# x load behind the zero fills, four first scatters on one table, one key wait per chunk, and a new penalty and reload order in the first attention

## The chip, the cores and the metric

The kernel runs on one core of a Trainium2 chip. The metric is device microseconds (us) of one execution, lower is better; three runs give a median, and one further execution was profiled. The engines are named as in the profile: PE (matmul), PEld (its weight load), DVE, ACT, POOL, and SP, which only issues transfers; SPq and ACTq are the queues that these two issue on.

## What is computed

Node features `x` (1024 x 512) pass four residual blocks: a graph attention, a mixture of 8 experts, a graph convolution, and a transformer layer with experts of its own. The graph has 17408 edges (`src`, `dst`, self loops included). The change is in the first block and in the making of its adjacency matrix:

```
x = x + L0_gnn(layernorm(x))
q, k, v = xn @ Wq + bq, xn @ Wk + bk, xn @ Wv + bv
adj  = zeros(1024, 1024).at[src, dst].set(1.0)
a    = q @ k.T / sqrt(512)
a    = a * adj + (1 - adj) * (-1e6)
out  = softmax(a) @ v
```

The third block needs the number of times that each edge occurs (`segment_sum` over repeated edges), so the kernel makes counts once and keeps them in DRAM.

## The kernel before

**Edges.** Edge e lies at partition p, column c (136 columns, in 34 "quads" of 4). A key `src * 1024 + dst` is compared with those of the same column on PE and DVE (`quad`), which turns an edge that occurs twice in a column into one leader with a count; `leaders` writes `index` and `count` for 2 quads at a time (the first 10 quads) or 3 quads at a time (the other 24) and raises `edges_ready` by that number. Each column is then one indirect transfer of 128 values that POOL issues (L447) and that adds `count` into a table of 1024 x 1024 floats in DRAM. There are two tables, so that a transfer need only wait for the one before the last: column c goes to table c % 2 and waits until column c - 2 has landed (`scattered[r]`). A table is cleared by a 4 MB transfer of zeros (L265) and a 512-byte one for a spare row (L267), both on SP's queue; `tables_clear[r]` counts them. SP's queue holds, in order: src, dst, the zeros of table 0, its spare row, the zeros of table 1, its spare row, two biases, four weight blocks. ACT issues the load of x as its first instruction.

**Projections.** DVE first does 10 quads, then waits for x, takes the layernorm (L795 to L820), and the halves of the first weights (WL). PE transposes the normalised x (L1213), then does the projections, with 3 quads ahead of each of 8 column blocks, and the scores q k^T, which ACT writes to `SR` (L573). Sums are made of three products of split operands (L237).

**First attention.** After the last scatter SP loads rows of both tables, 128 rows of the matrix (a tile t) at a time, into `CT[:, par, 0]` and `CT[:, par, 1]`, par = t % 2 (L321, `count_in`). POOL adds them (L474, `summed`), then makes the penalty 1e6 * min(count, 1) in `CT[:, par, 1]` (L476, `penalty`). DVE: m1 = min(count, 1) * SR (L908), m2 = (penalty - 1e6) + m1 (L913), the row maximum (L916). ACT: exp (L619). PE transposes the result (L1281), ACT copies that (`p_hi`, PTH), DVE takes the rest (`p_lo`, PTL, L787), PE multiplies with v (`values`), DVE adds to x (`residual`, L931) and takes statistics. The order on DVE is mask(t+2), p_lo(t+1), residual(t); on ACT softmax(t+2), p_hi(t+1). SP stores the summed counts (L325, `count_out`, `stored`) and loads tile t + 2 into the buffers of tile t once exp(t) and the store of t are done:

```
                wait(A["summed"], 2 * i + par + 1)
                count_out(2 * i + par, par)
                wait(A["exp"], 2 * i + par + 1)
                wait(A["stored"], 32 * i + 16 * par + 16)
                count_in(2 * i + par + 2, par)
```

Of the kernel before, what the change touches and what calls it, by code (L numbers as in the profile page):

```python
# [21 lines left out]
ALU = mybir.AluOpType  # L22
ACT = mybir.ActivationFunctionType
# [3 lines left out]
P = 128  # L27
# [6 lines left out]
def build(nc, a, out, ctx):  # L34
# [5 lines left out]
    EC = NE // P  # L40
# [3 lines left out]
    NH, DH = 8, D // 8  # L44
    NEG = 1000000.0
    TABLES = 2
    QUADS = EC // 4
    assert EC % 4 == 0 and HB == 2 and GB == 8 and NT == 8 and KT == 4

# [197 lines left out]
    def _(sp):  # L247
        def wait(s, value):

            sp.wait_ge(s, value)  # L250
            if not isinstance(value, int):
                sp.nop(nofuse=True)
# [11 lines left out]
        for r in range(TABLES):  # L264
            sp.dma_start(tables[r][0:N * N, :].rearrange("(p c f) o -> p c (f o)", p=P, c=4),  # L265
                         zeros[:, :].unsqueeze(1).to_broadcast([P, 4, 2048])).then_inc(tables_clear[r], 16)
            sp.dma_start(tables[r][N * N:N * N + P, :], zeros[:, 0:1]).then_inc(tables_clear[r], 16)  # L267
        with nc.allow_non_contiguous_dma(reason="biases, one feature per partition"):
            sp.dma_start(bq0[:, :], a["L0_gnn_bq"].rearrange("(k p) -> p k", p=P)).then_inc(cols0_in, 16)
            sp.dma_start(bk0[:, :], a["L0_gnn_bk"].rearrange("(k p) -> p k", p=P)).then_inc(cols0_in, 16)  # L270
# [43 lines left out]


        for r in range(TABLES):
            wait(scattered[r], 32 * QUADS)

        def count_in(t, par):
            for r in range(TABLES):  # L320
# [9 lines left out]
        with sp.Fori(0, NT // 2 - 1) as i:  # L330
            for par in range(2):
                wait(A["summed"], 2 * i + par + 1)
                count_out(2 * i + par, par)
                wait(A["exp"], 2 * i + par + 1)
                wait(A["stored"], 32 * i + 16 * par + 16)
                count_in(2 * i + par + 2, par)
        for t in (NT - 2, NT - 1):
# [74 lines left out]
    def _(gp):  # L412
# [23 lines left out]
                allow_small_or_imprecise_dtypes=True).then_inc(setup, 1)  # L436


        for r in range(TABLES):
            wait(tables_clear[r], 32)  # L440
        for q in range(QUADS):
            wait(edges_ready, q + 1)
            for c in range(4 * q, 4 * q + 4):
                r = c % TABLES
                if c >= TABLES:
                    wait(scattered[r], 16 * (c // TABLES))
                gp.indirect_dma_start(  # L447
                    out=tables[r], out_offset=bass.IndirectOffsetOnAxis(ap=index[:, c:c + 1], axis=0),
                    in_=count[:, c:c + 1], in_offset=None, compute_op=ALU.add).then_inc(scattered[r], 16)
# [20 lines left out]
        with gp.Fori(0, NT // 2) as i:  # L470
            for par in range(2):
                t = 2 * i + par
                wait(A["c_in"][par], 32 * i + 32)
                gp.tensor_tensor(CT[:, par, 0, :], CT[:, par, 0, :], CT[:, par, 1, :], ALU.add).then_inc(A["summed"], 1)  # L474
                wait(A["summed"], t + 1)
                gp.tensor_scalar(CT[:, par, 1, :], CT[:, par, 0, :], 1.0, NEG, ALU.min, ALU.mult).then_inc(A["penalty"], 1)  # L476

        def moe_split(which, u0, skip_first):
            if not skip_first:
# [85 lines left out]
    def _(act):  # L565
# [22 lines left out]
            copy(WH[:, slot, :], RAW[:, raw, :], w_hi)  # L588


        act.dma_start(X[:, :, :], a["x"].rearrange("(t p) d -> p t d", p=P)).then_inc(x_in, 16)
        root(0)
        for u in range(4):
            w_hi_of(u, 0, u, u)
# [17 lines left out]
            copy(SR[:, t, :], banks(4 + 2 * (t % 2)), Q0["s_done"], scale=D ** -0.5)  # L612


        def softmax(half, par):
            t = 2 * half + par
            act.wait_ge(A["mx"], t + 1)
            act.wait_ge(A["t_ps"][par], half)
            act.activation(PR[:, par, :], CT[:, par, 3, :], ACT.Exp, bias=neg_max[:, par:par + 1],  # L619
                           accum_out=denom[:, par:par + 1]).then_inc(A["exp"], 1)  # L620

        def p_hi(half, par):
            act.wait_ge(A["t_ps"][par], half + 1)
            act.wait_ge(A["av_ps"][par], half)
            copy(PTH[:, par, :], banks(4 + 2 * par), A["t_hi"][par])

        softmax(0, 0)
        softmax(0, 1)
        p_hi(0, 0)
        with act.Fori(0, NT // 2 - 1) as i:  # L630
            softmax(i + 1, 0)
            p_hi(i, 1)
            softmax(i + 1, 1)
            p_hi(i + 1, 0)
        p_hi(NT // 2 - 1, 1)
# [148 lines left out]
    def _(v):  # L784
# [118 lines left out]
        def mask(half, par):  # L903

            t = 2 * half + par
            v.wait_ge(A["summed"], t + 1)
            v.wait_ge(Q0["s_done"], NT)
            v.scalar_tensor_tensor(out=CT[:, par, 2, :], in0=CT[:, par, 0, :], scalar=1.0,  # L908
                                   in1=SR[:, ds(t), :].rearrange("p a n -> p (a n)"),
                                   op0=ALU.min, op1=ALU.mult).then_inc(A["m1"], 1)  # L910
            v.wait_ge(A["m1"], t + 1)
            v.wait_ge(A["penalty"], t + 1)
            v.scalar_tensor_tensor(out=CT[:, par, 3, :], in0=CT[:, par, 1, :], scalar=NEG, in1=CT[:, par, 2, :],  # L913
                                   op0=ALU.subtract, op1=ALU.add).then_inc(A["m2"], 1)
            v.wait_ge(A["m2"], t + 1)
            v.tensor_reduce(out=neg_max[:, par:par + 1], in_=CT[:, par, 3, :], axis=X_AXIS, op=ALU.max,  # L916
                            negate=True).then_inc(A["mx"], 1)
# [670 lines left out]
```

## Time and profile before

| | |
|---|---|
| three runs | 1388.9, 1382.31, 1389.77 us, median 1388.9 |
| profiled execution | 1383.41 us, span of its records 1381.6 us |
| busy share of the span | PE 77%, PEld 61%, DVE 49%, ACT 27%, POOL 49% |
| granted clock of PE, mean | 0.882 of full speed |

The busy shares are means over stages with different limits. No engine is busy all the time, so what a change in a stage is worth is read in that stage, from what each engine waits for there.

### The profile page before, as it was taken

To read this page: it belongs to the slowest core of one execution; us is meant where nothing else is said; L and a number is where in the kernel's file an instruction comes from. 1 tells how busy PE (TensorE), PEld (TensorE's weight loads), DVE (VectorE), ACT (ScalarE), POOL (GpSimd) and SP (SyncE) were. 2 spreads that over 40 slices of the span, in tenths; PEclk is the share of its full clock that TensorE was granted. 3 is DMA by queue.
4 is the path that set the end of the run, shared out by engine and by line. 5 is a ranking of instruction groups with operands and counts; after the bars stand their busy time and mean duration, and the time that the engine had idled before them with its cause. 6 is when DMAs were issued, how large, how long until landed. Compare 5 with 4: busy or idle time off the path is not lost.

```text
span 1381.6 us, 14502 instructions
## 1 busy us (share of the span) xinstructions
PE 1067.3 (77%) x4784; PEld 837.3 (61%) x4784; DVE 682.7 (49%) x1231; ACT 369.8 (27%) x536; POOL 670.7 (49%) x429
## 2 busy tenths in 40 slices
PE   3576797003878999995889878999998754999994
PEld 2455685002654788884678656777776633588883
DVE  6544320004763333455512466777877777243448
ACT  0201111001223121212221036656665522212120
POOL 1687888887632243210532036776856633233430
PEclk9977799555887899997999979999999995899997
DMA  9534222224521011002321031010000031111101
GB/s 307 63 24 26 8 1 1 0 12 156 182 77 30 16 53 53 23 0 87 99 58 39 15 100 30 16 46 17 23 16 16 0 122 46 31 46 46 46 0 61
DMA packets 79841, 68.86 MB, mean 50 GB/s; under 512 B 32288, under 2 KB 63264, under 8 KB 78512
## 3 DMA queue, kind: packets, MB, share of 16 engines
q1 hardware_dynamic: 59168, 66.06, 16.5%
q0 software_dynamic: 19584, 0.08, 4.2%
q10 hardware_dynamic: 1040, 2.10, 0.5%
q8 instruction: 28, 0.46, 0.1%
q14 instruction: 21, 0.17, 0.0%
HBM read 47.17 MB, written 16.85 MB: 46 GB/s over the span
## 4 chain that ended last, share of the span: by engine, by line
PE 52%; DVE 18%; POOL 14%; issue 7%; DMA 6%; ACT 3%; SPq 0%; DVEq 0%; ACTq 0%; POOLq 0%
PE PS L237 40%; POOL edge_table L447 13%; DMA edge_table<-zeros 3%; DMA edge_table<-count,index 3%; DVE neg_max L1119 2%; PE PS L1452 2%; PE PS L1467 2%; PE PS L1441 2%; DVE APL L787 2%; PE PS L1466 2%; PE PS L1357 2%; DVE stats L795 1%; DVE XN L820 1%; DVE XN L1187 1%; PE PS L1213 1%
## 5 line engine op out<-in xcount | busy, mean ns | idle before, releaser
L459 POOL CAST WH<-RAW 128x512 fp32r<-128x512 f32 x94 | 65.5, 696 | 466.8 <-PE PS L237 370.1
L447 POOL DMA_INDIRECT edge_table<-count,index x136 | 214.9, 1580 | 87.0 <-issue 42.0
L537 POOL TENSOR_SCALAR AP__133<-AP__133,rden 128x1024 f32<-128x1024 f32 x64 | 181.9, 2847 | 84.9 <-DVE rden L1124 84.2
L237 PE MATMUL PS<-XTH,WH 128*128 128x512 f32 x480 | 169.8, 421 | 8.9 <-DVE XTL L787 6.7
L237 PE MATMUL PS<-XTL,WH 128*128 128x512 f32 x480 | 164.4, 409 | 0.0
L237 PE MATMUL PS<-XTH,WL 128*128 128x512 f32 x480 | 162.2, 404 | 0.0
L461 POOL TENSOR_TENSOR WL<-RAW,WH 128x512 fp32r<-128x512 f32 x94 | 138.2, 1470 | 12.1 <-POOL WH L459 0.8
L787 DVE TENSOR_TENSOR HL<-HF,HH 128x1024 fp32r<-128x1024 f32 x32 | 46.9, 1468 | 174.4 <-ACT HH L573 174.4
L237 PEld LDWEIGHTS PS<-XTH,WH 128*128 128x128 f32 x480 | 95.2, 201 | 32.8 <-issue 12.4
L237 PEld LDWEIGHTS PS<-XTL,WH 128*128 128x128 f32 x480 | 96.6, 201 | 20.8
L655 ACT ACTIVATE HF<-PS,b 128x1024 f32<-128x1024 f32 x32 | 35.7, 1117 | 272.0 <-PE PS L237 272.0
L237 PEld LDWEIGHTS PS<-XTH,WL 128*128 128x128 f32 x480 | 95.2, 198 | 21.4
L237 PE MATMUL PS<-WH,HH 128*128 128x512 f32 x256 | 99.6, 389 | 0.0
L237 PE MATMUL PS<-WL,HH 128*128 128x512 f32 x256 | 99.6, 389 | 0.0
L237 PE MATMUL PS<-WH,HL 128*128 128x512 f32 x256 | 99.6, 389 | 0.0
L1119 DVE TENSOR_REDUCE neg_max<-PS 128x1 f32<-128x1024 f32 x64 | 78.2, 1222 | 36.2 <-PE PS L1441 35.3
L787 DVE TENSOR_TENSOR APL<-PS,APH 128x512 fp32r<-128x512 f32 x128 | 82.9, 678 | 23.3 <-ACT APH L573 23.2
L1281 PE MATMUL PS<-ident,PR 128*128 128x128 f32 x64 | 11.2, 333 | 104.5 <-ACT PR L619 104.5
L573 ACT ACTIVATE APH<-PS 128x512 fp32r<-128x512 f32 x128 | 71.7, 597 | 67.4 <-PE PS L1452 43.0
L1213 PE MATMUL PS<-ident,XN 128*128 128x128 f32 x128 | 30.8, 417 | 67.1 <-DVE XTL L787 33.3
L1452 PE MATMUL PS<-ident,AP__133 128*128 128x128 f32 x512 | 70.8, 280 | 11.3 <-DVE APL L787 10.8
L1452 PEld LDWEIGHTS PS<-ident,AP__133 128*128 128x128 f32 x512 | 59.6, 143 | 26.9 <-issue 17.0
(189 smaller groups left out, 2013.1 us busy)
## 6 DMA issues: line engine op xcount, KB each, us to landing
edge_table<-zeros SPq DMA_DIRECT2D x2, 4096.0 KB, 28.0
RAW<-in_L_ffn_w SPq DMA_DIRECT2D x32, 256.0 KB, 2.7
CT<-edge_table SPq DMA_DIRECT2D x16, 512.0 KB, 5.0
RAW<-in_L_ffn_W SPq DMA_DIRECT2D x32, 256.0 KB, 2.8
counts<-CT SPq DMA_DIRECT2D x8, 512.0 KB, 6.0
CG<-counts SPq DMA_DIRECT2D x8, 512.0 KB, 3.3
RAW<-in_L_gnn_W SPq DMA_DIRECT2D x16, 256.0 KB, 2.7
edge_table<-count,index POOLq DMA_INDIRECT x136, 3.0
```

Source lines behind the costliest of these rows:

```text
L237: got = pe.matmul(o, lhs, r, start=first and j == 0, stop=last and j == 2)
L447: gp.indirect_dma_start(out=tables[r], out_offset=bass.IndirectOffsetOnAxis(ap=index[:, c:c + 1], axis=0), in_=count[:, c:c + 1], in_offse ...
L459: gp.tensor_copy(wh, RAW[:, raw, :]).then_inc(w_hi, 1)
L461: gp.tensor_tensor(wl, RAW[:, raw, :], f(wh), ALU.subtract).then_inc(w_ready, 1)
L537: gp.tensor_scalar(AP_[:, i % 4, :], AP_[:, i % 4, :], rden[:, i % 4:i % 4 + 1], None, ALU.mult).then_inc(B["norm"], 1)
L573: act.activation(dst, src, Copy, **kw).then_inc(s, 1)
L655: act.activation(HF[:, b, :], banks(2 * b), ACT.Gelu, bias=b1[:, ds(2 * e + b)]).then_inc(M["gelu"][b], 1)
L787: v.tensor_tensor(dst, src, f(hi), ALU.subtract).then_inc(s, 1)
L1119: v.tensor_reduce(out=neg_max[:, i % 4:i % 4 + 1], in_=banks(2 * (i % 2)), axis=X_AXIS, op=ALU.max, negate=True).then_inc(B["mx"], 1)
L1213: got = pe.transpose(PS[:, t % 2, k * P:(k + 1) * P], src[:, t, k * P:(k + 1) * P], ident[:, :])
L1357: pe.matmul(PS[:, 4 + t % 4, :], gatesT[0:NEXP, t * P:(t + 1) * P], b2[:, which, :], start=True, stop=True).then_inc(M["g_ps"], 1)
L1452: got = pe.transpose(PS[:, 4 + half, k * P:(k + 1) * P], AP_[:, i % 4, c * P:(c + 1) * P], ident[:, :])
```

## The change

1. The load of x is taken from ACT's queue and put on SP's, behind the zeros of both tables.
2. Columns 0 to 3 are all added into table 0; from column 4 on the tables alternate as before. The first transfer waits for table 0 alone, and column 5, the first of table 1, waits for that table. SP's two final counts follow (70 transfers on table 0, 66 on table 1).
3. POOL waits for `edges_ready` once for each group of 2 or 3 quads (13 waits), not at each of 34 quads.
4. The penalty is made by ACT as relu(1 - count), ahead of each exp, and DVE's m2 is now (relu * -1e6) + m1. DVE's m2(t) also waits for exp(t-2), which reads the buffer that it writes.
5. SP loads tile t + 2 after m2(t) in place of exp(t). The store of t is still waited for.

```diff
--- before.py
+++ after.py
@@ -44,6 +44,7 @@
     NH, DH = 8, D // 8
     NEG = 1000000.0
     TABLES = 2
+    FIRST = 4
     QUADS = EC // 4
     assert EC % 4 == 0 and HB == 2 and GB == 8 and NT == 8 and KT == 4
 
@@ -265,6 +266,7 @@
             sp.dma_start(tables[r][0:N * N, :].rearrange("(p c f) o -> p c (f o)", p=P, c=4),
                          zeros[:, :].unsqueeze(1).to_broadcast([P, 4, 2048])).then_inc(tables_clear[r], 16)
             sp.dma_start(tables[r][N * N:N * N + P, :], zeros[:, 0:1]).then_inc(tables_clear[r], 16)
+        sp.dma_start(X[:, :, :], a["x"].rearrange("(t p) d -> p t d", p=P)).then_inc(x_in, 16)
         with nc.allow_non_contiguous_dma(reason="biases, one feature per partition"):
             sp.dma_start(bq0[:, :], a["L0_gnn_bq"].rearrange("(k p) -> p k", p=P)).then_inc(cols0_in, 16)
             sp.dma_start(bk0[:, :], a["L0_gnn_bk"].rearrange("(k p) -> p k", p=P)).then_inc(cols0_in, 16)
@@ -314,7 +316,7 @@
 
 
         for r in range(TABLES):
-            wait(scattered[r], 32 * QUADS)
+            wait(scattered[r], 8 * (EC - FIRST) + 16 * FIRST * (1 - r))
 
         def count_in(t, par):
             for r in range(TABLES):
@@ -331,7 +333,7 @@
             for par in range(2):
                 wait(A["summed"], 2 * i + par + 1)
                 count_out(2 * i + par, par)
-                wait(A["exp"], 2 * i + par + 1)
+                wait(A["m2"], 2 * i + par + 1)
                 wait(A["stored"], 32 * i + 16 * par + 16)
                 count_in(2 * i + par + 2, par)
         for t in (NT - 2, NT - 1):
@@ -436,14 +438,17 @@
                 allow_small_or_imprecise_dtypes=True).then_inc(setup, 1)
 
 
-        for r in range(TABLES):
-            wait(tables_clear[r], 32)
+        into = [0] * FIRST + [c % TABLES for c in range(FIRST, EC)]
+        chunk_starts = set(range(0, 10, 2)) | set(range(10, QUADS, 3))
         for q in range(QUADS):
-            wait(edges_ready, q + 1)
+            if q in chunk_starts:
+                wait(edges_ready, q + 1)
             for c in range(4 * q, 4 * q + 4):
-                r = c % TABLES
-                if c >= TABLES:
-                    wait(scattered[r], 16 * (c // TABLES))
+                r, turn = into[c], into[:c].count(into[c])
+                if turn:
+                    wait(scattered[r], 16 * turn)
+                else:
+                    wait(tables_clear[r], 32)
                 gp.indirect_dma_start(
                     out=tables[r], out_offset=bass.IndirectOffsetOnAxis(ap=index[:, c:c + 1], axis=0),
                     in_=count[:, c:c + 1], in_offset=None, compute_op=ALU.add).then_inc(scattered[r], 16)
@@ -472,8 +477,6 @@
                 t = 2 * i + par
                 wait(A["c_in"][par], 32 * i + 32)
                 gp.tensor_tensor(CT[:, par, 0, :], CT[:, par, 0, :], CT[:, par, 1, :], ALU.add).then_inc(A["summed"], 1)
-                wait(A["summed"], t + 1)
-                gp.tensor_scalar(CT[:, par, 1, :], CT[:, par, 0, :], 1.0, NEG, ALU.min, ALU.mult).then_inc(A["penalty"], 1)
 
         def moe_split(which, u0, skip_first):
             if not skip_first:
@@ -588,7 +591,6 @@
             copy(WH[:, slot, :], RAW[:, raw, :], w_hi)
 
 
-        act.dma_start(X[:, :, :], a["x"].rearrange("(t p) d -> p t d", p=P)).then_inc(x_in, 16)
         root(0)
         for u in range(4):
             w_hi_of(u, 0, u, u)
@@ -612,6 +614,11 @@
             copy(SR[:, t, :], banks(4 + 2 * (t % 2)), Q0["s_done"], scale=D ** -0.5)
 
 
+        def no_edge(half, par):
+            t = 2 * half + par
+            act.wait_ge(A["summed"], t + 1)
+            act.activation(CT[:, par, 1, :], CT[:, par, 0, :], ACT.Relu, bias=1.0, scale=-1.0).then_inc(A["penalty"], 1)
+
         def softmax(half, par):
             t = 2 * half + par
             act.wait_ge(A["mx"], t + 1)
@@ -624,12 +631,16 @@
             act.wait_ge(A["av_ps"][par], half)
             copy(PTH[:, par, :], banks(4 + 2 * par), A["t_hi"][par])
 
+        no_edge(0, 0)
+        no_edge(0, 1)
         softmax(0, 0)
         softmax(0, 1)
         p_hi(0, 0)
         with act.Fori(0, NT // 2 - 1) as i:
+            no_edge(i + 1, 0)
             softmax(i + 1, 0)
             p_hi(i, 1)
+            no_edge(i + 1, 1)
             softmax(i + 1, 1)
             p_hi(i + 1, 0)
         p_hi(NT // 2 - 1, 1)
@@ -910,8 +921,9 @@
                                    op0=ALU.min, op1=ALU.mult).then_inc(A["m1"], 1)
             v.wait_ge(A["m1"], t + 1)
             v.wait_ge(A["penalty"], t + 1)
-            v.scalar_tensor_tensor(out=CT[:, par, 3, :], in0=CT[:, par, 1, :], scalar=NEG, in1=CT[:, par, 2, :],
-                                   op0=ALU.subtract, op1=ALU.add).then_inc(A["m2"], 1)
+            v.wait_ge(A["exp"], t - 1) if t >= 2 else None
+            v.scalar_tensor_tensor(out=CT[:, par, 3, :], in0=CT[:, par, 1, :], scalar=-NEG, in1=CT[:, par, 2, :],
+                                   op0=ALU.mult, op1=ALU.add).then_inc(A["m2"], 1)
             v.wait_ge(A["m2"], t + 1)
             v.tensor_reduce(out=neg_max[:, par:par + 1], in_=CT[:, par, 3, :], axis=X_AXIS, op=ALU.max,
                             negate=True).then_inc(A["mx"], 1)
```

How the change moves instructions is shown at three places. First SP's queue at the start of the program (the names are tiles and inputs; `zeros` is the source of the fills). Before:

```order
L265 DMA edge_table0<-zeros_98 512x1x2048 [waits zeros_set]
L267 DMA edge_table0<-zeros_98 128x1
L265 DMA edge_table1<-zeros_98 512x1x2048
L267 DMA edge_table1<-zeros_98 128x1
L269 DMA bq0_60<-in_L0_gnn_bq 128x4x1
L270 DMA bk0_61<-in_L0_gnn_bk 128x4x1
L258 DMA RAW_84<-in_L0_gnn_Wq 128x4x128
```

And in the changed kernel:

```order
L266 DMA edge_table0<-zeros_98 512x1x2048 [waits zeros_set]
L268 DMA edge_table0<-zeros_98 128x1
L266 DMA edge_table1<-zeros_98 512x1x2048
L268 DMA edge_table1<-zeros_98 128x1
L269 DMA X_87<-in_x 128x8x512
L271 DMA bq0_60<-in_L0_gnn_bq 128x4x1
L272 DMA bk0_61<-in_L0_gnn_bk 128x4x1
L259 DMA RAW_84<-in_L0_gnn_Wq 128x4x128
```

x is now the fifth transfer of that stretch, ahead of the biases and of every weight. Second, POOL at its first scatters. Before:

```order
L447 DMA edge_table0<-count_112,index_111 1048704x1 [waits edges_ready,table1_clear,table0_clear]
L447 DMA edge_table1<-count_112,index_111 1048704x1
L447 DMA edge_table0<-count_112,index_111 1048704x1 [waits scattered0]
L447 DMA edge_table1<-count_112,index_111 1048704x1 [waits scattered1]
L447 DMA edge_table0<-count_112,index_111 1048704x1 [waits scattered0,edges_ready]
```

And in the changed kernel:

```order
L452 DMA edge_table0<-count_112,index_111 1048704x1 [waits table0_clear,edges_ready]
L452 DMA edge_table0<-count_112,index_111 1048704x1 [waits scattered0] x4
L452 DMA edge_table1<-count_112,index_111 1048704x1 [waits table1_clear]
L452 DMA edge_table0<-count_112,index_111 1048704x1 [waits scattered0]
L452 DMA edge_table1<-count_112,index_111 1048704x1 [waits scattered1]
```

The wait for table 1 has moved from the first transfer to the sixth, and columns 1 to 4 each wait for the landing of the one just before. Third, ACT at the start of the first attention (SR is the copy of the scores, PR the exp, PTH the copy of its transpose). Before:

```order
L573 ACTIVATE SR_90<-PS 128x1024 x8
L619 ACT_TABLE_LOAD
L619 ACTIVATE PR_100,denom_82<-CT_99,neg_max_81 128x1024 x2
L573 ACTIVATE PTH_101<-PS 128x1024
L630 UNCONDITIONAL_BRANCH
```

And in the changed kernel:

```order
L576 ACTIVATE SR_90<-PS 128x1024 x8
L620 ACTIVATE CT_99<-CT_99 128x1024 x2
L626 ACT_TABLE_LOAD
L626 ACTIVATE PR_100,denom_82<-CT_99,neg_max_81 128x1024 x2
L576 ACTIVATE PTH_101<-PS 128x1024
L639 UNCONDITIONAL_BRANCH
```

The two new activations of tiles 0 and 1 stand between the scores and the table load of exp, so that this load no longer follows the scores at once; inside the loop behind it no further table load appears.

## Rows read from the trace of the kernel before

**Rows 1.** The page, chain that ended last, shares by line.

```profile
PE PS L237 40%; POOL edge_table L447 13%; DMA edge_table<-zeros 3%; DMA edge_table<-count,index 3%; DVE neg_max L1119 2%; PE PS L1452 2%; PE PS L1467 2%; PE PS L1441 2%; DVE APL L787 2%; PE PS L1466 2%; PE PS L1357 2%; DVE stats L795 1%; DVE XN L820 1%; DVE XN L1187 1%; PE PS L1213 1%
```

**Rows 2.** The chain in time, 0 to 60 us: start, length, what.

```profile
3.35 0.83 SPq L267
...
4.93 36.31 DMA edge_table<-zeros
```

**Rows 3.** Transfers by issue, first 4 us: KB each, us from issue to landing.

```profile
X<-in_x ACTq DMA_DIRECT2D x1, 2048.0 KB, 16.7
...
edge_table<-zeros SPq DMA_DIRECT2D x1, 0.5 KB, 23.3
```

**Rows 4.** Busy time by stretch; the last columns are PEclk, DMA share, GB/s.

```profile
9.00:19.00 10.00, 6.90 (x52) 5.00 (x52) 7.47 (x52) 0.00 (x0) 0.00 (x0) 1.00 1.01 423
```

**Rows 5.** Timeline of POOL, scatters; in brackets idle before and releaser.

```profile
42.16 1.78 POOL L447 DMA_INDIRECT edge_table<-count,index  x1 [37.28 <-DMA edge_table<-zeros]
44.24 2.05 POOL L447 DMA_INDIRECT edge_table<-count,index  x1 [0.30 <-issue]
46.85 1.55 POOL L447 DMA_INDIRECT edge_table<-count,index  x1 [0.56 <-DMA edge_table<-count,index]
49.50 1.55 POOL L447 DMA_INDIRECT edge_table<-count,index  x1 [1.11 <-DMA edge_table<-count,index]
...
55.06 1.55 POOL L447 DMA_INDIRECT edge_table<-count,index  x1 [0.30 <-issue]
...
305.25 1.55 POOL L447 DMA_INDIRECT edge_table<-count,index  x1 [0.30 <-issue]
```

**Rows 6.** Groups by line on POOL, 41 to 308 us.

```profile
L447 POOL DMA_INDIRECT edge_table<-count,index x136 | 214.9, 1580 | 87.0 <-issue 42.0 <-DMA edge_table<-zeros 37.3 <-DMA edge_table<-count,index 7.7
```

**Rows 7.** Timeline of DVE and ACT around the projections and scores.

```profile
35.09 3.74 DVE L820 TENSOR_SCALAR XN<-X,mv,rstd 128x512 f32<-128x512 f32 x8
...
54.10 0.69 DVE L787 TENSOR_TENSOR XTL<-PS,XTH 128x512 fp32r<-128x512 f32 x1 [0.16 <-ACT XTH L573]
...
231.75 1.02 ACT L573 ACTIVATE SR<-PS 128x1024 f32<-128x1024 f32 x1 [4.41 <-PE PS L237]
232.79 1.28 ACT L619 ACT_TABLE_LOAD   x1
```

**Rows 8.** Timeline of the first attention's start, all engines.

```profile
313.44 2.34 POOL L474 TENSOR_TENSOR CT<-CT 128x1024 f32<-128x1024 f32 x1 [2.77 <-DMA CT<-edge_table]
315.96 4.63 POOL L476 TENSOR_SCALAR CT<-CT 128x1024 f32<-128x1024 f32 x1 [0.18 <-POOL CT L474]
...
321.05 3.03 DVE L913 SCALAR_TENSOR_TENSOR CT<-CT 128x1024 f32<-128x1024 f32 x1 [3.96 <-POOL CT L476]
...
325.37 1.15 ACT L619 ACTIVATE PR<-CT,neg_max 128x1024 f32<-128x1024 f32 x1 [91.30 <-DVE neg_max L916]
...
326.99 0.83 SPq L321 DMA_DIRECT2D CT<-edge_table  x2
...
333.21 2.36 POOL L474 TENSOR_TENSOR CT<-CT 128x1024 f32<-128x1024 f32 x1 [5.64 <-DMA CT<-edge_table]
...
335.61 1.22 DVE L908 SCALAR_TENSOR_TENSOR CT<-CT,SR 128x1024 f32<-128x1024 f32 x1 [2.02 <-POOL CT L474]
...
346.26 0.74 DVE L931 SCALAR_TENSOR_TENSOR X<-PS,rden,X 128x512 f32<-128x512 f32 x1
```

**Rows 9.** Timeline of DVE, one later round of the loop.

```profile
356.55 1.20 DVE L908 SCALAR_TENSOR_TENSOR CT<-CT,SR 128x1024 f32<-128x1024 f32 x1
...
362.49 1.22 DVE L787 TENSOR_TENSOR PTL<-PS,PTH 128x1024 fp32r<-128x1024 f32 x1 [2.15 <-ACT PTH L573]
...
365.23 1.21 DVE L908 SCALAR_TENSOR_TENSOR CT<-CT,SR 128x1024 f32<-128x1024 f32 x1
```

**Rows 10.** Transfers issued from 344 to 346 us, landing times.

```profile
CT<-edge_table SPq DMA_DIRECT2D x2, 512.0 KB, 4.9
counts<-CT SPq DMA_DIRECT2D x1, 512.0 KB, 6.2
```

## The prediction, made before the changed kernel was run

> **What bounds the kernel now.** I read the chain that ended last first: the products lead it, but the scatters (L447) hold 13% of it and the zero fills 3% [rows 1]. The chain in time says how: the fill of table 1 and its spare row, issued at 4.93, land 36.31 later, at 41.24 [rows 2], and the first scatter starts at 42.16 after 37.28 idle on that wait [rows 5]. From there POOL issues a scatter every 1.85 us (1.55 and 0.30 of issue), the last at 305.25 [rows 5]. DVE and PE are no part of this: POOL's idle time before its 136 scatters is issue, the fill and scatter landings, never DVE's keys [rows 6]. ACT copies the last scores at 231.75 and has nothing to do for 91 us until the first exp at 325.37 [rows 7, 8]. So a microsecond off the start of the scatters is one off the end, and PE's projections have some 70 us to spare.
>
> In the first attention two things take turns. At its start the masks wait for POOL: m2(0) waited 3.96 for the penalty (4.63 on POOL) and then took 3.03 beside POOL's next sum, tile 2 is only reloaded at 326.99, after exp(0), and m1(2) starts at 335.61 when POOL has summed it [rows 8]. Later m1 starts every 8.68 us (356.55, 365.23) with no wait ahead of it; the one gap on DVE is 2.15 us, for ACT's exp and copy [rows 9]. That loop (DVE's 6.5 us of work for a tile and ACT's 2.2 between) is its own bound and doesn't contain the reload.
>
> **x behind the fills.** x (2048 KB) and table 0's zeros run together: x lands 16.7 after its issue at 0.81, table 0's spare row at 3.35 + 23.3 = 26.65 [rows 2, 3]. The 16 DMA engines move 423 GB/s then, with a share of 1.01, so they are full [rows 4]. Without x table 0 is clear 2.10 MB / 423 GB/s = 5.0 us earlier, at 21.7, and table 1 at 36.2. x itself then follows table 1 and lands at about 41, not 17.5. The load that was hidden behind DVE's quads now isn't: DVE needs about 6 us for the statistics, 1 for the root and 3.74 for XN [rows 7], so XN is done near 53, not 38.8. The split transposes (XTL, done at 54.8 before [rows 7]) end near 65, and PE's stage ends 10 us later, at some 243. The scatters end near 298: this costs nothing, and would only begin to above a delay of about 60 us. The keys of column 40 and on come 10 us later too; no wait of POOL names DVE today [rows 6], and POOL needs column 40 after 40 scatters, beyond 100 us.
>
> **Four scatters on one table.** The first scatter can start at 21.7 + 0.9 (as 42.16 follows 41.24) = 22.6. Each of the next four waits for the landing of the one before. What that costs under load shows at the first two: scatter 2, behind 0, started 4.7 after it (42.16 to 46.85), scatter 3 behind 1 5.3 after it (44.24 to 49.50) [rows 5]. I take 5.0 between starts: 22.6, 27.6, 32.6, 37.6, 42.6 for columns 0 to 4. Column 5 goes 1.85 later, at 44.5, when table 1 is long clear, and column 6 waits for 4, at 47.6. Before, column 6 started at 55.06 [rows 5]. From there the old rhythm goes on: 7.5 us earlier. The bounds: in the quiet stretch a scatter two places behind finds the earlier one landed (idle 0.30), so 3.7 between starts is enough there [rows 5], which makes column 6 start at 41.1, 14 us earlier; at 6.5 us between starts the gain of the start is nothing.
>
> **A page speaks against this.** x took 16.7 us beside the fill [rows 3] where its bytes alone need 5.0 at 423 GB/s [rows 4]: whatever shares the engines with the zeros is stretched threefold. The Trainium skill ("DMA: Bandwidth & Descriptors", Queues, rings and completion order) says that each DMA engine goes round its queues and drains a packet of some 9 to 17 descriptors from one before the next. With rows of 8 KB an estimate from that page is 3 to 5 us more for every landing beside the fill, and nearly all of the 7.5 us gone. I hold it as a rival below.
>
> **One key wait per chunk.** Of the 42.0 us idle put to issue [rows 6], 0.30 each is the floor [rows 5]. Read scatter by scatter, the 21 quads whose wait goes had 3.7 us above that floor at their first scatter; two of them (1.3 and 0.8) are no key waits by their size. That leaves 1.6, the term that I take; bounds 0 and 3.7.
>
> **Penalty and reload.** Times on the old scale, with sum(0) from 313.44 to 315.78 [rows 8]. Removed from POOL: eight penalties of about 4 us (4.63 the first). Added on ACT: eight relus of 128x1024, priced by exp at 1.15 [rows 8]; ACT has 6 us idle in each round, since DVE's loop holds it. relu(0) runs beside m1(0), so m2(0) starts near 317.2. Sum(1) is now on POOL at once, not at 320.66, so I let m2(0) pay the 3.03 that it paid beside a sum before: done at 320.2, not 324.1. The table load of exp (1.28 [rows 7]), formerly hidden at 232.79, now comes after relu(1), which needs sum(1), done near 319.5: 320.7 to 322.0. Max(0) is done at 321.4, so it shows by some 0.5 us on exp(0); exp(1) waits for max(1) at 325.2 anyhow, and PTH(0) stands behind exp(1), so it costs nothing on the path. If sum(1) were 3 us later it would cost all of that.
> Reload of tile 2: 0.5 after m2(0), at 320.7 where it was 326.99; the store of tile 0, alone in the queue, is long done. Sum(2) starts 6.2 after the issue as before (326.99 to 333.21), ends at 329.3, and m1(2) starts there in place of 335.61. From m1 to the residual the loop takes 5.94 and 1.14 (356.55 to 362.49, then PTL) = 7.1 where nothing waits [rows 9]; before, it took 10.65 here (335.61 to 346.26 [rows 8]), since m2(2) waited for POOL. So residual(0) is at 336.4 in place of 346.26: 9.8 us earlier. PE's product of tile 0 starts near 329 and is not the last to be ready.
> From there on nothing more comes: the loop stays at 8.68 a tile. The reload could also go no faster than the store lets it: 6.2 for the store behind two loads [rows 10], 0.83 to issue the loads [rows 8] and some 0.4 between are 7.4 a tile, which is below 8.68, so it is hidden but by only 1.3. Against that, sums now fall at other points of DVE's loop; one that meets a two-operand DVE instruction cost 1.8 us (3.03 for 1.2 [rows 8, 9]). With four sums and DVE busy 6.5 of 8.68, of which a third is of that kind, I take off 1.6. Term: 8.2, bounds 3 (every sum collides) and 11.5 (none, and m2(0) at 1.2).
>
> **The sum.** 7.5 + 1.6 + 8.2 = 17.3 us against the profiled execution's 1383.41: 1366.1. The runs shown lie at 1382.3, 1388.9 and 1389.8, so the profiled one is near the lowest and the median 5.5 above it; I round up towards that: 1367. About 0.5% (7 us) is what a measurement of this kernel can tell from no change.
>
> **The rivals.**
> A, the forecast: 1359 to 1373. Chance 0.55.
> B, landings beside the fill take 8.5 us, as x's stretching and the page suggest: columns 0, 1, 2 at 22.6, 31.1, 39.6, then 5.0 apart, column 6 at 54.6, 0.5 us gained at the start, 1373.1. Against it: the scatters have 128 values, x a thousand rows. Chance 0.18.
> C, landings stay near 3.4: column 6 at 41.1, 14 us, 1359.6. Against it: 5.3 is measured while weights load. Chance 0.12.
> D, the earlier reload doesn't do what it says, because sums hit DVE's masks or relu(t+2) holds ACT ahead of a copy: attention term 3, 1371.3. Chance 0.07.
> E, slower: the chain of same-table scatters beside a full queue stretches so far that it outweighs the rest. Price 5 x spacing for column 6; the start loses above 6.5 us between starts, the whole turns 0.5% slower at 9.8 (column 6 at 71.6, 16.5 lost against 9.8 gained). At 11 us: column 6 at 77.6, 1396. No scatter of the trace before is near that (5.3 the longest seen at the start). Chance 0.04.
> F, B and D together: within 0.5%, 1378. Chance 0.04.
> The range takes in A, most of B, C and D and the 5 us between executions: 1356 to 1377. Faster by over 0.5% needs 1376.5 or less: A, C and most of B and D, 0.88. Within it: F and the rest of B and D, 0.08. Slower: E, 0.04.
>
> **What would show it.** First scatter near 22 to 23 (5.0 right), starts 5.0 apart, column 6 near 47.6; last scatter near 296; x landed near 41 and the last score copy near 242, with no wait of POOL for DVE. In the attention: reload of tile 2 some 7.3 us after sum(0) begins (13.6 before), m1(2) 16 after it (22.2 before), residual(0) 23 after it (32.8 before), and m1 then 8.7 apart. Wrong would be: spacings above 6, m1 above 9 apart, or table loads between exps.

## The result, and the profile after

The changed kernel takes 1379.57 us (median of 10, 1376.97 to 1383.6) against 1389.38 (median of 10, 1382.31 to 1393.82) for the kernel before: ratio 0.9935, 95% interval [0.9917, 0.9953]. It is faster, by 9.8 us at the medians, where 17.3 were forecast, and 1379.57 lies above the range that ended at 1377. On two more chips the same kernel gave 0.9937 [0.9915, 0.9958] and 0.9931 [0.9913, 0.9949].

The chain that ended last, by line (answers to [rows 1]):

```profile
PE PS L238 40%; POOL edge_table L452 13%; DMA edge_table<-count,index 5%; DVE neg_max L1131 3%; PE PS L1479 2%; PE PS L1464 2%; DVE APL L798 2%; PE PS L1478 2%; PE PS L1453 2%; PE PS L1369 2%; DVE stats L806 1%; DVE XN L831 1%; DVE CT L925 1%; DVE XN L1199 1%; PE PS L1225 1%
```

The landings of the scatters have risen from 3% to 5%, and the 3% of zero fills are no longer named. They have shrunk, not gone: the first scatter still waited for table 0, clear at 23.05, and the profile names DVE's keys only because one of their instructions ended later, at 23.71:

```profile
23.95 1.77 POOL L452 DMA_INDIRECT edge_table<-count,index  x1 [18.99 <-DVE index L873]
```

Those were keys of columns 32 to 39; the keys of column 0 had been written at 9.7, and the third profile of this kernel names the fill, with 1% of the chain. One wait has in the main taken the place of another. The chain in time shows which, at the start of the changed kernel (start, length, what; with [rows 2]):

```profile
23.95 11.58 DMA edge_table<-count,index
35.53 0.27 issue
35.80 9.05 DMA edge_table<-count,index
44.85 0.27 issue
45.12 5.01 DMA edge_table<-count,index
50.12 0.27 issue
50.39 2.97 DMA edge_table<-count,index
```

The first scatter does start 18.2 us earlier than the 42.16 of [rows 5]. But it takes 11.58 us to land (from its start until its arrival is signalled), the next 9.05, then 5.01 and 2.97, and each waits for the one before. The timeline of POOL has what comes of it:

```profile
57.33 3.38 POOL L452 DMA_INDIRECT edge_table<-count,index  x1 [0.31 <-issue]
...
309.48 1.55 POOL L452 DMA_INDIRECT edge_table<-count,index  x1 [0.30 <-issue]
```

57.33 is column 6, which started at 55.06 before [rows 5]: all of the 18 us, and 2.3 more, are lost by there. The landing times of the transfers issued from 2 to 7 us (three answers, KB and us to landing; with [rows 3]):

```profile
edge_table<-zeros SPq DMA_DIRECT2D x1, 4096.0 KB, 15.2
```

```profile
edge_table<-zeros SPq DMA_DIRECT2D x1, 0.5 KB, 19.7
```

```profile
edge_table<-zeros SPq DMA_DIRECT2D x1, 4096.0 KB, 29.7
X<-in_x SPq DMA_DIRECT2D x1, 2048.0 KB, 38.8
edge_table<-zeros SPq DMA_DIRECT2D x1, 0.5 KB, 35.6
```

The two 0.5 KB rows were issued at 3.35 and 5.10: table 0 is clear at 23.05 (26.65 before), table 1 at 40.7 (41.24 before). x, issued at 6.54, is in at 45.3. So the first landing (11.58) ran beside the fill of table 1, the second (9.05) beside that table's spare row and x, the third (5.01) beside the first weights, and the fourth (2.97) beside nothing. The stretches (last columns PEclk, DMA share, GB/s; with [rows 4]) show a hole behind the first fill:

```profile
4.00:14.00 10.00, 6.55 (x48) 4.69 (x48) 6.68 (x44) 0.00 (x0) 0.96 (x5) 1.00 1.01 414
16.00:22.00 6.00, 3.36 (x25) 2.34 (x24) 4.73 (x33) 0.00 (x0) 0.00 (x0) 1.00 0.40 15
```

15 GB/s from 16 to 22 us: the fill's data is nearly all gone by 16, and something small holds the queue for 6 us. The trace of the kernel before has the same hole, a little later:

```profile
21.00:26.00 5.00, 2.22 (x16) 1.56 (x16) 4.30 (x32) 0.00 (x0) 0.00 (x0) 1.00 0.83 54
```

In the first attention the timeline (all engines; with [rows 8]) is what was forecast, nearly to the tenth:

```profile
317.63 2.34 POOL L479 TENSOR_TENSOR CT<-CT 128x1024 f32<-128x1024 f32 x1 [2.73 <-DMA CT<-edge_table]
...
321.52 3.04 DVE L925 SCALAR_TENSOR_TENSOR CT<-CT 128x1024 f32<-128x1024 f32 x1 [0.24 <-DVE CT L919]
...
324.59 1.28 ACT L626 ACT_TABLE_LOAD   x1
...
324.94 0.83 SPq L323 DMA_DIRECT2D CT<-edge_table  x2
...
333.37 1.23 DVE L919 SCALAR_TENSOR_TENSOR CT<-CT,SR 128x1024 f32<-128x1024 f32 x1 [0.46 <-POOL CT L479]
...
340.47 0.74 DVE L943 SCALAR_TENSOR_TENSOR X<-PS,rden,X 128x512 f32<-128x512 f32 x1
```

Counted from the first sum (317.63): the reload at 7.3, m1(2) at 15.7, residual(0) at 22.8, where 7.3, 16 and 23 were forecast and 13.6, 22.2 and 32.8 stood before. Then the gain shrinks again, in two rounds of DVE's loop (with [rows 9]):

```profile
359.43 1.21 DVE L919 SCALAR_TENSOR_TENSOR CT<-CT,SR 128x1024 f32<-128x1024 f32 x1
360.67 3.29 DVE L925 SCALAR_TENSOR_TENSOR CT<-CT 128x1024 f32<-128x1024 f32 x1
```

```profile
360.33 2.54 POOL L479 TENSOR_TENSOR CT<-CT 128x1024 f32<-128x1024 f32 x1 [4.87 <-DMA CT<-edge_table]
```

POOL's sum starts just ahead of m2, and m2 takes 3.29 in place of 1.22. Nearly the same happens a round later.

The two profiled executions, stage by stage (us, from start to start):

| stage | before | after |
|---|---|---|
| to the start of column 6 | 55.06 | 57.33 |
| to the last scatter | 250.19 | 252.15 |
| to the first sum | 8.19 | 8.15 |
| to the last exp | 73.25 | 68.41 |
| to the root of the next layernorm | 18.28 | 19.60 |
| the rest | 976.63 | 974.96 |
| span | 1381.6 | 1380.6 |

The rest, which the change doesn't touch, differs by up to 7.6 us among the thirteen profiles of this document (971.78 to 979.41), so the span of one profile is a poor measure of a change. The profiled execution of before was 6 us below the median of its runs and the one after 2.8 above its own, so their difference understates the change; two later profiles of the changed kernel have spans of 1374.4 and 1368.5. From here on times are compared by ratios, against runs of the kernel before on the same chip, and places in the program by profiles.

### The profile page after: what moved, and what is told of

The parts are those of the page before. It is cut to its first block, busy times and chain, and to the rows that moved or that the text cites. A ratio compares the mean times of both kernels' runs of the same rounds, so it can differ in the third digit from the quotient of the medians.

```text
span 1380.6 us, 14465 instructions
## 1 busy us (share of the span) xinstructions
PE 1063.4 (77%) x4784; PEld 834.1 (60%) x4784; DVE 688.0 (50%) x1231; ACT 377.8 (27%) x544; POOL 642.9 (47%) x421
## 4 chain that ended last, share of the span: by engine, by line
PE 52%; DVE 19%; POOL 14%; DMA 6%; issue 6%; ACT 3%; DVEq 0%; SPq 0%; ACTq 0%; POOLq 0%
PE PS L238 40%; POOL edge_table L452 13%; DMA edge_table<-count,index 5%; DVE neg_max L1131 3%; PE PS L1479 2%; PE PS L1464 2%; DVE APL L798 2%; PE PS L1478 2%; PE PS L1453 2%; PE PS L1369 2%; DVE stats L806 1%; DVE XN L831 1%; DVE CT L925 1%; DVE XN L1199 1%; PE PS L1225 1%
## 5 line engine op out<-in xcount | busy, mean ns | idle before, releaser
L1225 PE MATMUL PS<-ident,XN 128*128 128x128 f32 x128 | 31.4, 425 | 84.3 <-DVE XN L831 40.7
L1225 PEld LDWEIGHTS PS<-ident,XN 128*128 128x128 f32 x128 | 23.8, 219 | 91.7 <-DVE XN L831 44.0
```

What stands on the lines that cost most here:

```text
L1225: got = pe.transpose(PS[:, t % 2, k * P:(k + 1) * P], src[:, t, k * P:(k + 1) * P], ident[:, :])
```

## The experiments

Theory 1: the new start gives nothing, because scatters on one table wait for landings that the full queue stretches; the gain is that of the attention part and the key waits. Rivals: the start does gain in executions without a profile; or the first scatters are slow by themselves; or the fills' end (the spare rows) is what holds them.

**The attention part alone.** The kernel before with the relu penalty and the reload after m2:

```diff
-                wait(A["exp"], 2 * i + par + 1)
+                wait(A["m2"], 2 * i + par + 1)
+            act.activation(CT[:, par, 1, :], CT[:, par, 0, :], ACT.Relu, bias=1.0, scale=-1.0).then_inc(A["penalty"], 1)
```

> Only the attention part of the change (relu penalty on ACT, reload of tile t+2 after m2(t)); x, the tables, the scatters and the key waits are those of before. Theory 1 (the attention part carries the whole gain, the new start gives nothing back): scatter 0 at 42.2, last scatter at 305, from the first table sum to the last exp 68 to 69 us in place of 73.3, time 4 to 6 us below before. Rival (the start gains too, outside of what one profile shows): this kernel gains clearly less than half of what the whole change gained (9.8 us), that is under 4 us.

Measured: 1377.94 against 1382.8, ratio 0.9955 [0.9937, 0.9973], which is 6.2 us less. From the first sum (315.32) to the last exp (381.43) 66.1 us in place of 73.25, 7.1 less where 4 to 5 were expected: one late m2 of 3.3, where the profile of the whole change has two. Theory 1 holds for this part, though it isn't the whole gain.

**The new start alone.** x behind the fills and four scatters on table 0, all else as before:

```diff
+        sp.dma_start(X[:, :, :], a["x"].rearrange("(t p) d -> p t d", p=P)).then_inc(x_in, 16)
+        into = [0] * FIRST + [c % TABLES for c in range(FIRST, EC)]
```

> Only the move of x and the four first scatters on table 0; key waits and attention are those of before. Theory 1 (landings beside the fills cost more than the earlier start brings): scatter 0 near 24, starts of columns 0 to 4 about 12, 9, 5 and 3 us apart, column 6 near 57 in place of 55.1, last scatter 2 to 5 us later than 305.3, time 2 to 5 us above before. Rival (the profiled execution was an unlucky one): column 6 before 50, last scatter before 300, time 5 to 8 us below before.

Measured: 1386.59 against 1382.8, ratio 1.0023 [1.0005, 1.0041]: 3.2 us slower. POOL's timeline:

```profile
23.34 1.78 POOL L450 DMA_INDIRECT edge_table<-count,index  x1 [18.30 <-DMA edge_table<-zeros]
38.34 1.56 POOL L450 DMA_INDIRECT edge_table<-count,index  x1 [13.22 <-DMA edge_table<-count,index]
44.99 1.55 POOL L450 DMA_INDIRECT edge_table<-count,index  x1 [5.08 <-DMA edge_table<-count,index]
```

Column 1 starts 15.0 after column 0, column 6 at 57.22, the last scatter at 309.27 (305.25 before). The start as changed is a loss on its own.

**x alone.** Only the load of x moved behind both fills:

> Only x moved behind both fills; columns alternate between the tables from the first and wait for both tables, as before. If x beside the fill of table 0 was what kept the tables late, both are clear 5 us earlier and scatter 0 starts at 37, last scatter near 300, time 5 us below before. If the two writes of 512 bytes for the spare rows stall the queue for a length of their own that absorbs part of it (6 us before, 7 to 8 us in the changed kernel), table 1 is clear at 38 to 39 and the gain is 2 to 3 us.

Measured: 1382.54 against 1382.8, ratio 1.0008 [0.9991, 1.0024], no difference. The first scatter starts at 40.59:

```profile
40.59 1.78 POOL L448 DMA_INDIRECT edge_table<-count,index  x1 [35.66 <-DMA edge_table<-zeros]
42.67 1.57 POOL L448 DMA_INDIRECT edge_table<-count,index  x1 [0.30 <-issue]
47.08 1.55 POOL L448 DMA_INDIRECT edge_table<-count,index  x1 [2.83 <-DMA edge_table<-count,index]
```

Taking 2 MB from beside the fills brings 1.6 us, not 5.0 (2.7 against the first scatter of the attention part alone, 43.28), and x, now beside the first scatters, takes it back: column 2 waits 2.83 for column 0, whose landing took 6.2. The last scatter starts at 305.37. In run time no gain is seen, less than the 2 to 3 us of the second expectation.

**The second fill held back.** The changed kernel, but SP waits for the four scatters before it issues the fill of table 1:

```diff
         for r in range(TABLES):
+            if r:
+                wait(scattered[0], 64)
```

> The changed kernel, but SP issues the fill of table 1, and with it x and the weights, only after the four first scatters have landed. If the landings are slow because a full queue shares the DMA engines with them, columns 0 to 3 start 3.2 to 3.5 us apart (first near 24, fourth landed near 37). If the first scatters are slow by themselves, or because of the spare row of table 0, the first still takes 9 to 12 us to land. The fill starts about 20 us later than in the changed kernel, so the whole is some 10 to 15 us slower than the changed kernel by either theory.

Measured: ratio 0.9974 [0.9953, 0.9995] (1380.04 against 1382.8). POOL's timeline:

```profile
21.46 1.77 POOL L454 DMA_INDIRECT edge_table<-count,index  x1 [16.51 <-DMA edge_table<-zeros]
24.96 1.56 POOL L454 DMA_INDIRECT edge_table<-count,index  x1 [1.72 <-DMA edge_table<-count,index]
28.25 1.55 POOL L454 DMA_INDIRECT edge_table<-count,index  x1 [1.73 <-DMA edge_table<-count,index]
31.56 1.55 POOL L454 DMA_INDIRECT edge_table<-count,index  x1 [1.76 <-DMA edge_table<-count,index]
```

With the queue quiet the same scatters on the same table are 3.3 to 3.5 us apart in place of 11.9, 9.3 and 5.3. That is the cause: it is what shares the DMA engines with them, not the scatters and not table 0. The edit holds back x and the weights together with the fill, so it doesn't say how much each of them adds. The last part of the expectation was wrong: by ratios from different chips this kernel loses some 5 us against the changed one (2 to 9 with the intervals), not 10 to 15, and column 6 starts at 57.80 in place of 57.33. Filling table 1 beside the scatters had won half a microsecond at column 6 over filling it after them.

**The key waits alone.**

```diff
-            wait(edges_ready, q + 1)
+            if q in chunk_starts:
+                wait(edges_ready, q + 1)
```

> Only the key waits: 13 in place of 34, all else as before. The scatters' extra idle at the first column of the 21 quads goes: 1.5 to 2 us from column 8 to the last scatter (246.4 before). If the parts of the change simply add (attention -6.2, start +3.2, whole -9 on two chips), the key waits would have to be worth some 6 us, which the idle times of the profile do not hold: then the time falls by 5 us or more. If the profile has all of it: 1 to 2.5 us below before.

Measured: 1381.65 against 1384.97, ratio 0.9976 [0.9962, 0.999], 3.3 us less. The scatters' group (busy, mean ns, idle before; with [rows 6]) has 39.3 of issue in place of 42.0:

```profile
L449 POOL DMA_INDIRECT edge_table<-count,index x136 | 214.8, 1579 | 84.3 <-issue 39.3 <-DMA edge_table<-zeros 37.3 <-DMA edge_table<-count,index 7.7
```

From column 8 to the last scatter it is 244.1 in place of 246.4. The measured time lies between the two expectations; the profile holds 2 to 3 us of it, and the interval of the runs goes from 1.4 to 5.3.

**All but the new start.** The changed kernel with x on ACT's queue and alternating columns, beside the changed kernel on the same chip:

> The changed kernel without its new start: x on ACT's queue, columns alternating from the first, both tables waited for; key waits and attention as changed. If the new start costs 2 to 3 us (columns 0 to 4 one behind the other beside the fill), this kernel is 1 to 3 us faster than the changed one, 10 to 12 us below before. If the start is worth something in unprofiled executions that the profiles don't show, it is slower than the changed kernel: 5 to 8 us below before.

> The changed kernel once more, on the same chip as the two kernels above, so that they are compared with it directly: 8 to 10 us below before as on two chips, and column 6 between 56 and 58.

Measured: without the new start 1376.12, ratio 0.993 [0.9912, 0.9947]; with it 1375.45, ratio 0.9931 [0.9913, 0.9949]. Column 6 starts at 56.20 in the one and at 55.55 in the other, the last scatter at 304.11 and 305.82. The new start is worth nothing here, within some 3 us either way. It was 3.2 us slower alone (0.7 to 5.7); the two intervals overlap, so all that can be said is that it costs between nothing and some 3 us. The first repeat, on another chip, said the same of the whole:

> The changed kernel itself once more, beside a run of the kernel before on this chip. Its parts alone gave 6.2 us (attention), minus 3.2 us (start) and by reading the scatters some 1.5 us (key waits): 4.5 us together, where the whole was measured at 9.8 us. If the parts add up, this one is 3 to 6 us below before. If it is 8 us or more below again, the parts don't add and something of the whole is missing in them. The spread of the first scatters should stay: column 1 some 12 to 15 us after column 0.

Measured: 1378.39 against 1387.53, 0.9937, which is 9.1 us less and so on the side of "the parts don't add". With the key waits measured (3.3 in place of the 1.5 read from the trace) most of the gap closes: the parts' ratios multiplied (0.9955, 0.9976, 1.0023) give 0.9954, the whole 0.9931 to 0.9937; each part is uncertain by 0.0014 to 0.0018, so the gap of 0.002 that is left isn't shown to be one.

**The spare rows.** The changed kernel with the 128 spare values written from one partition, as one row:

```diff
-            sp.dma_start(tables[r][N * N:N * N + P, :], zeros[:, 0:1]).then_inc(tables_clear[r], 16)
+            sp.dma_start(tables[r][N * N:N * N + P, :].rearrange("f o -> o f"), zeros[0:1, 0:P]).then_inc(tables_clear[r], 16)
```

> The changed kernel with the spare row of each table written by one row of 128 values from one partition, in place of 128 values of 4 bytes from 128 partitions. If the 4-byte writes are what leaves the DMA engines nearly idle for 6 to 7 us after each fill (8 to 49 GB/s from 16 to 23 us), table 0 is clear near 18 and table 1 near 29, x lands near 34, and column 6 starts 8 to 12 us earlier than in the changed kernel (57.3), time 8 to 12 us below it. If the pause belongs to the end of a 4 MB fill (its write receipts) and not to the spare row, nothing moves by more than 2 us.

Measured: 1365.1 against 1387.53, ratio 0.9844 [0.9826, 0.9862]; that is 13.3 us less than the changed kernel on the same chip, more than the 8 to 12 expected. The stretch that ran at 15 GB/s is full:

```profile
16.00:22.00 6.00, 3.33 (x25) 2.33 (x24) 4.98 (x33) 0.00 (x0) 1.46 (x1) 1.00 1.02 422
```

And POOL's first scatters:

```profile
15.68 1.77 POOL L452 DMA_INDIRECT edge_table<-count,index  x1 [10.76 <-DMA edge_table<-zeros]
26.32 1.56 POOL L452 DMA_INDIRECT edge_table<-count,index  x1 [8.87 <-DMA edge_table<-count,index]
32.98 1.55 POOL L452 DMA_INDIRECT edge_table<-count,index  x1 [5.10 <-DMA edge_table<-count,index]
```

Table 0, fill and row together, is clear at 14.76, so the pause isn't the end of the fill. With the 128 separate values and nothing behind them (the kernel that holds the second fill back) it is clear at 20.54, 5.8 later, after 6 us at 0 GB/s.

The first scatter starts 8.4 earlier than in the changed kernel on that chip (24.06), column 6 12.3 earlier (44.27, 56.54), the last scatter 9.8 earlier (296.01, 305.85). The trace has no more than that for the new rows: the other 3.5 us of the 13.3 lie within what the rest of the program varies by. The landings beside the fill and then x are about as slow as before, 10.6 and 6.7 between starts; they only come earlier. x is in at 5.84 + 26.9 = 32.7.

**Sums held.** The changed kernel with POOL's sum of tile t held until the maximum of tile t - 1:

```diff
+            if t >= 3:
+                wait(A["mx"], t)
```

> The changed kernel with POOL's sum of tile t (from tile 3 on) held until the row maximum of tile t-1, so that it falls into DVE's wait for ACT. Theory (a sum that starts as m2 is due costs DVE 2 us each time): m2 stays at 1.23 for every tile from 1 on, from sum(0) to the last exp 63.3 us in place of 68.4, time about 3 to 5 us below the changed kernel. Rival (the longer rounds come from the reload or from ACT's added relu): no m2 above 1.3, but rounds of 10 us remain and the time does not move.

Measured: 1374.88 against 1387.53, ratio 0.9912 [0.9894, 0.9929], 3.5 us below the changed kernel. From first sum to last exp 63.0 us. One round:

```profile
353.58 2.36 POOL L480 TENSOR_TENSOR CT<-CT 128x1024 f32<-128x1024 f32 x1 [6.32 <-DVE neg_max L929]
...
355.72 1.22 DVE L799 TENSOR_TENSOR PTL<-PS,PTH 128x1024 fp32r<-128x1024 f32 x1 [2.15 <-ACT PTH L577]
...
358.47 1.20 DVE L920 SCALAR_TENSOR_TENSOR CT<-CT,SR 128x1024 f32<-128x1024 f32 x1
359.70 1.23 DVE L926 SCALAR_TENSOR_TENSOR CT<-CT 128x1024 f32<-128x1024 f32 x1
```

The sum runs in DVE's 2.15 us wait for ACT, and no m2 from tile 1 on is above 1.23. The rounds are 8.68 again, so neither the reload nor the added relu had made them longer. The kernel that holds the second fill back says the same by luck: there no sum happened to fall just ahead of a late m1 or m2, and it has 63.3 us without any hold.

**Together.** x behind both fills, one-row spare writes, alternating columns, 13 key waits, held sums:

> x behind both fills, one-row spare writes, columns alternating from the first with both tables waited for (no four scatters on one table), 13 key waits, the new attention with held sums. If the start is bound by bytes (8.4 MB of zeros at 425 GB/s) once the 4-byte writes are gone, scatter 0 starts near 27, column 6 near 41 (two or three landings of 5 to 6 us beside x), last scatter near 290, and the time is 20 to 27 us below before. If the pauses are not the spare rows', scatter 0 starts near 39 and the time is 10 to 13 us below before.

Measured: 1360.23 against 1387.53, ratio 0.9798 [0.978, 0.9816], 27.3 us below before.

```profile
26.73 1.77 POOL L451 DMA_INDIRECT edge_table<-count,index  x1 [21.76 <-DMA edge_table<-zeros]
28.80 1.56 POOL L451 DMA_INDIRECT edge_table<-count,index  x1 [0.30 <-issue]
33.11 1.55 POOL L451 DMA_INDIRECT edge_table<-count,index  x1 [2.74 <-DMA edge_table<-count,index]
```

Waiting for both tables from the first column and alternating, the scatters start 11 us later than with the spare rows alone (15.68), and column 6 starts 3.5 us earlier (40.76 against 44.27). The last scatter starts at 294.39, not near 290, 1.6 before that of the spare rows alone. x behind the fills stayed in this version; with x ahead of them it wasn't tried. This is the fastest kernel here; that of the spare rows alone also beats both, before and after.

## Why the prediction was wrong

**What bounds the kernel**: right. The scatters, once started, set the end of the stage in every profile, and PE's projections never did: the last score copy ended near 245.2 (ACT had idled 74.75 when the first relu came at 320.00). No scatter waited for its keys: in all thirteen profiles the first scatter of each group of 2 or 3 quads starts at least 6 us after the index of that group was written, and where DVE's index is named as the releaser it is that of a later group.

**x behind the fills**: the free part was right (x landed at 45.3, not 41, and DVE waited 21.65 us for it, which PE's 75 us of slack took in), the size of the gain was not. I took 5.0 us off both tables by bytes. Measured: table 0 is clear 3.6 earlier, table 1 0.5 earlier, and with x alone moved the first scatter came 1.6 earlier. The step treated the queue as bound by bytes, from the one stretch at 423 GB/s, and passed over the next, 54 GB/s from 21 to 26 us, in the same trace. The 512-byte spare rows aren't bound by bytes: 128 values of 4 bytes from 128 partitions hold the queue for some 6 us (15 GB/s from 16 to 22). The kernel with one-row writes shows it. Whether they write slowly or complete slowly no run separates.

**Four scatters on one table**: this is the step that failed. I took 5.0 us between starts, from the landings of [rows 5], which ran beside weight loads at a third to a half of the full rate. Beside the full-rate fill the first took 11.9, beside spare row and x the second 9.3; the third and fourth, 5.3 and 3.2, came near the price or under it. With the fill held back all are 3.3 to 3.5. The term that x and this step share was +7.5 of gain and measured between 0 and -3 us, column 6 at 57.33 where 47.6 was forecast. My rival B had the mechanism (landings stretched beside the fill) and a price of 8.5 us; I gave it 0.18, for the scatters' small size, and size turned out not to protect them. The Trainium skill's rule ("DMA: Bandwidth & Descriptors", Queues, rings and completion order), that a DMA engine drains a packet of 9 to 17 descriptors from one queue before it turns to the next, pointed the right way: by the estimate from it 3 to 5 us more for a landing. The trace has about 8 more (11.6 against 3.2), so the size isn't explained by one such turn. The page also says that a semaphore's write lands only after every earlier write of that engine, across its queues; that would add the fill's outstanding writes to each landing, and no run here shows it apart. What rows show is that a landing doesn't wait for the whole fill: in the kernel with held sums column 0 landed at 32.7, 1.8 before table 1's fill was in (4.00 + 30.5 = 34.5). What sets the 11.6 stays open.

**One key wait per chunk**: right in kind, 1.6 forecast, 3.3 measured; the interval (1.4 to 5.3) has the 1.6 in it, and the profile shows 2 to 3.

**Penalty and reload**: right, 8.2 forecast, 6.2 measured at the medians (3.7 to 8.7) and 7.1 in its profile. The start of the stage was right to 0.3 us at three places. The deduction of 1.6 for sums that meet m1 or m2 was a third of what they cost here (m1 or m2 took 3.3 to 3.4 where 1.2 is usual, in one or two of the last rounds, and 1.5 to 2.3 in the last: 5.2 us in the profile of the changed kernel, 0.3 to 3.1 in six others), and which rounds are hit changes from one profile to the next. In the first hit m2, from 360.67, ends at 363.96, 1.1 after the end of POOL's sum (360.33 + 2.54 = 362.87), which is nearly a whole m2. So DVE didn't share, it waited. The Trainium skill ("SBUF — State Buffer", SBUF: two separate sides) says this: a DVE instruction with two SBUF inputs and a GpSimd one take turns at a shared port for a whole instruction. The trace agrees, in the other order too: the next sum, started at 370.48 while m1 ran (370.18 to 371.39), took 3.15 in place of 2.34. No table load came between exps, and the one that was moved stood where I put it.

**The sum**: 6.2 + 3.3 and a start worth nothing make 9.5, the whole measured 9.8. Of the 12.6 us between 1367 and 1379.57, 7.5 are missing gain, the start's term (attention 2.0 short and key waits 1.7 over nearly cancel), and 5.1 are the base: I subtracted from the profiled execution, 1383.41, and rounded up by 0.9 only, where the median of ten runs is 1389.38. From that median even the full 17.3 would have given 1372.1, and B, priced at 1373.1 with its start at +0.5, would have been 1379, in part by luck: B had column 6 at 54.6, and it came at 57.33. The range was too narrow at the upper end for both reasons.

## What to carry to other kernels

A transfer whose completion is waited for must be priced by landings beside the same load that it will meet, not by landings of a quieter stretch; a chain of such transfers beside a full queue is worth avoiding, and an earlier start is no gain if it only moves the chain into that load. Look at the rate of the queue in small stretches before counting its bytes: a hole behind each large transfer, here from 512 bytes each, was worth at least as much as everything the change did (13.3 us by the runs and 9.8 by the trace, against 9.1 for the change on the same chip). When work is taken from one engine, ask where its remaining instructions now fall in the other engines' loops, and place them in a wait on purpose.

## What was not expected of the hardware

- 128 writes of 4 bytes to DRAM from 128 partitions hold a queue that runs at 414 GB/s down to 15 GB/s for 6 us; with the same 512 bytes from one partition it moves 422 to 431 GB/s in that stretch.
- A scatter of 128 values lands in about 3.2 us on a quiet queue, in 6.1 to 6.4 us beside the 2 MB load of x (three profiles), and in 11.6 us (9.0 to 14.7 in six profiles) when it is issued as a 4 MB fill begins beside it.
- A POOL sum of two 128x1024 f32 tiles that starts just ahead of DVE's m2 stretches m2 from 1.22 to between 3.0 and 3.4 us, while one that starts during m1 or m2 is itself stretched (2.5 to 3.5 for 2.34).
